# Scattering the rows of alternate expert tiles into two DRAM tensors, and adding the second to the first at the end

## What is computed

```python
x = x + xattn(ctx_1024, layernorm(x))            # 32 x 100 x 256, residual
z    = layernorm(x) * g + b
p    = softmax(z @ rW + rb)                       # 8 experts
topv, topi = top_k(p, 2)
w    = topv / sum(topv)                           # weights of the 2 experts of a row
hid  = gelu(z @ W1[e] + b1[e])                    # 256 -> 512, for each chosen e
y    = hid @ W2[e] + b2[e]                        # 512 -> 256
out  = x + sum over the 2 chosen e of w[e] * y
```

## Time and profile before

| | us |
|---|---|
| median of 3 runs | 854.98 |
| lowest and highest of the 3 | 854.52, 857.09 |
| the profiled execution: its own time | 857.09 |
| the profiled execution: span from first to last instruction | 855.3 |

### The profile page before, as it was taken

The page is one execution under the profiler, slowest core; times in us unless marked ns, Lnnn a source line. Parts: engine busy times, 40 slices in busy tenths (PEclk is TensorE's granted clock), DMA queues, the critical chain, the costliest instruction groups (busy, mean ns, idle before and its releaser), DMA issues.

```text
span 855.3 us, 26299 instructions
## 1 busy us (share of the span) xinstructions
PE 753.1 (88%) x8056; PEld 587.4 (69%) x8057; DVE 672.4 (79%) x1859; ACT 535.4 (63%) x1412; POOL 554.0 (65%) x610
## 2 busy tenths in 40 slices
PE   3389999999999999999999997655797698999994
PEld 2256677777777777777767675444687697988894
DVE  6389999999999999999999997993457865555562
ACT  2236788888888888888888885443363354554551
POOL 5432877777877777777778675433654457777773
PEclk9999999999999999999999999856999899999998
DMA  8846567677677576676776757611233233443341
GB/s 191 153 111 142 124 145 167 158 169 164 155 170 170 136 190 142 167 170 151 171 164 152 193 130 180 192 16 53 44 64 44 49 57 63 69 67 52 63 67 18
DMA packets 152792, 104.43 MB, mean 122 GB/s; under 512 B 68657, under 2 KB 147853, under 8 KB 152609
## 3 DMA queue, kind: packets, MB, share of 16 engines
q1 hardware_dynamic: 132598, 77.03, 39.6%
q0 software_dynamic: 11776, 16.15, 11.7%
q10 hardware_dynamic: 8362, 10.57, 4.3%
HBM read 36.65 MB, written 17.33 MB: 63 GB/s over the span
## 4 chain that ended last, share of the span: by engine, by line
PE 65%; DVE 15%; issue 7%; DMA 5%; DVEq 4%; POOL 3%; ACT 1%; ACTq 1%; POOLq 0%; SPq 0%
PE pj L863 10%; PE pj L832 9%; PE s_row L877 9%; PE zt L908 8%; PE s_t L896 8%; PE s_row L967 6%; DVE negmax L1336 3%; PE pj L850 3%; PE pj L978 3%; PE zt L978 2%; DMA q_stack<-q_part 2%; DVE v_neg L1442 1%; DVEq L1429 1%; DVEq L1437 1%; PE tr L932 1%
## 5 line engine op out<-in xcount | busy, mean ns | idle before, releaser
L1336 DVE TENSOR_REDUCE negmax<-s_row 100x1 f32<-100x361 f32 x512 | 251.4, 523 | 20.7 <-PE s_row L877 13.6
L1155 ACT ACTIVATE p_t<-s_t 128x400 f32<-128x400 f32 x384 | 188.6, 501 | 56.3 <-PE s_t L896 49.5
L877 PE MATMUL s_row<-stack_x,q_stack 125*128 125x361 bf16 x512 | 132.1, 320 | 15.7 <-DMA q_stack<-q_part 7.4
L703 POOL DMA_INDIRECT out_x<-v_neg,idx_s x57 | 94.2, 1652 | 75.6 <-DVE v_neg L1444 36.1
L896 PE MATMUL s_t<-q_stack,stack_x 128*128 128x100 bf16 x1536 | 128.7, 211 | 11.0 <-ACT p_t L1155 10.3
L896 PEld LDWEIGHTS s_t<-q_stack,stack_x 128*128 128x128 bf16 x1536 | 93.0, 99 | 57.3 <-issue 27.0
L967 PE MATMUL s_row<-w_qkv,v_aug 128*128 128x128 f32 x912 | 118.4, 285 | 13.7 <-DVE v_aug L1431 13.7
L967 PEld LDWEIGHTS s_row<-w_qkv,v_aug 128*128 128x128 f32 x912 | 111.6, 200 | 17.2 <-DVE v_aug L1431 14.8
L863 PE MATMUL pj<-w_qkv,ct 128*128 128x256 f32 x384 | 106.9, 402 | 0.0
L1141 ACT ACTIVATE w_qkv<-s_row,b_k 128x128 f32<-128x128 f32 x228 | 65.2, 369 | 63.0 <-PE s_row L967 63.0
L832 PE MATMUL pj<-ct,w_qkv 128*128 128x361 f32 x256 | 94.9, 494 | 10.8 <-DMA bk_s<-in_bk 9.7
(11 more groups left out here) (234 smaller groups left out, 1432.2 us busy)
## 6 DMA issues: line engine op xcount, KB each, us to landing
stack_x<-k_part SPq DMA_DIRECT2D x192, 192.0 KB, 3.8
q_stack<-q_part SPq DMA_DIRECT2D x186, 64.0 KB, 2.0
ct<-in_ctx_t SPq DMA_DIRECT2D x32, 361.0 KB, 4.9
stack_x<-in_w ACTq DMA_DIRECT2D x8, 512.0 KB, 6.2
w_s<-in_w ACTq DMA_DIRECT2D x14, 256.0 KB, 2.9
zscr<-zn SPq DMA_DIRECT2D x32, 100.0 KB
z_in<-zscr SPq DMA_DIRECT2D x32, 100.0 KB
zf_d<-zf_s SPq DMA_DIRECT2D x32, 100.0 KB
```

The lines of the kernel that those rows point to most:

```text
L703: pool.indirect_dma_start(out_rows[0:n], bass.IndirectOffsetOnAxis(idx_s[:, k.slot:k.slot + 1], 0), ys[:, k.slot, :], None, bounds_check=n ...
L877: nc.tensor.matmul(s_row[h % 2][:, 0:KEYS], q_stack[0:MROW, b.slot, h, :], k_stack[0:MROW, b.slot, h, 0:KEYS], start=True, stop=True).then ...
L1155: nc.scalar.activation(p_t[:, quad % 2, kt, :], s_t[g % 2][:, 0:4 * Q], ACT.Exp).then_inc(exp_done, 1)
L1336: v.tensor_reduce(negmax[:, b.slot, h:h + 1], s_row[h % 2][0:Q, 0:KEYS], AXIS.X, ALU.max, negate=True).then_inc(max_done, 1)
```

## The change

Scatters of even tiles still add to `out`; scatters of odd tiles now add to a second DRAM tensor, `odd_d`, of the same shape. Two transfers that follow each other thus never touch the same bytes, and scatters of one parity are ordered through DVE's step as before, so the wait on the other parity goes, together with the table `clear_at`, its two DVE instructions per group of tiles, its constants and POOL's register load. For this

- `odd_d` has to be zero at first: POOL writes 128 x 640 zeros over a dead part of `x_all` at the start of iteration 27, and ACT's queue sends them ten times over to `odd_d` (3.28 MB) at the start of iteration 29. ACT waits for that transfer at the start of iteration 31, POOL before the first scatter;
- at the end, after both parities have landed, POOL issues one DMA from DRAM to DRAM that adds all of `odd_d` to `out`, 400 rows of 2048 numbers (3.28 MB), and waits for it.

```diff
@@ zeroing (POOL, ACT)
+                    if isinstance(turn, int) and i == 27:
+                        pool.wait_ge(x2_stored, 16 * LOOSE)
+                        g.memset(zeros, 0.0).then_inc(zeros_ready, 1)
...
                 def load_weights(i):
+                    if i == 29:
+                        act.wait_ge(zeros_ready, 1)
+                        act.dma_start(odd_d.rearrange("b q d -> (b q d)").rearrange("(p r n) -> p r n", p=128, n=640),
+                                      zeros.unsqueeze(1).broadcast_to([128, B * Q * D // (128 * 640), 640])).then_inc(odd_zeroed, 16)
                     if i == 31:
+                        act.wait_ge(odd_zeroed, 16)
@@ first_gathers (POOL)
                     pool.wait_ge(x2_stored, 16 * LOOSE)
+                    pool.wait_ge(odd_zeroed, 16)
@@ scatter (POOL)
                 def scatter(k):
-                    other = scattered[1 - k.slot]
-                    if k.known and k.index in (3, NF):
-                        pool.wait_ge(clear_known, {3: 1, NF: 2}[k.index])
-                    if k.known and k.index in (0, 1, 2, NT - 1):
-                        after(pool, other, 16 * ((k.index + 1) // 2))
+                    if k.known:
+                        pool.wait_ge(y_ready, k.index + 1)
                     else:
-                        pool.reg_load(clear, clear_at[0:1, bass.ds(k.index, 1)])
-                        pool.wait_ge(other, clear)
-                    pool.wait_ge(y_ready, scatters[k.slot])
-                    pool.reg_add(scatters[1 - k.slot], scatters[k.slot], 1)
+                        pool.wait_ge(y_ready, scatters[k.slot])
+                        pool.reg_add(scatters[1 - k.slot], scatters[k.slot], 1)
                     n = rows_in(k)
-                    pool.indirect_dma_start(out_rows[0:n], ...
+                    pool.indirect_dma_start((out_rows, odd_rows)[k.slot][0:n], ...
@@ after the last scatter (POOL)
                 for k in range(2):
                     pool.wait_ge(scattered[k], 16 * len(range(k, NT, 2)))
+                wide = [t.rearrange("b q d -> (b q d)").rearrange("(r n) -> r n", n=2048) for t in (out, odd_d)]
+                pool.dma_start(wide[0], wide[1], accum_op=ALU.add, max_dma_last_dim=8192).then_inc(odd_added, 16)
+                pool.wait_ge(odd_added, 16)
@@ to_places (DVE)
-                    route(dve, v.tensor_tensor(same, te_i[:, mine], te_i[:, mine.start - 1:mine.stop - 1], ALU.is_equal))
-                    v.scalar_tensor_tensor(clear_at[0:Q, mine], same, -16.0, landed[:, mine.start - 3:mine.stop - 3], ALU.mult, ALU.add).then_inc(clear_known, 1)
```

More of the change, by code:

```diff
@@ L157, in build @@
 def build(nc, x, ctx_t, wq_t, bq, wk_t, bk, wv_t, bv, gamma, beta, ln_g, ln_b, rw, rb, w1, b1, w2, b2,
-          ident_d, route_c, zscr, zf_d, out):
+          ident_d, route_c, zscr, zf_d, odd_d, out):
     es = ExitStack()
@@ L224, in build @@
         ln0 = [ln0_all[:, k * B:k * B + B] for k in range(3)]
-        cst = stats_all[:, 0:E + 128 + 1 + NT - 3]
-        rev, lanes, query, landed = carve(cst, (E, 128, 1, NT - 3))
+        cst = stats_all[:, 0:E + 128 + 1]
+        rev, lanes, query = carve(cst, (E, 128, 1))
         ones, earlier = carve(ln0_all[:].bitcast(BF16), (Q, Q))
@@ L265, in build @@
         b2_s = ct[:].rearrange("p a c k -> p (a c k)")[:, 0:E * D].rearrange("p (e f) -> p e f", e=E)
-        w2_loaded, cst_loaded, clear_known = sem("w2_loaded"), sem("cst_loaded"), sem("clear_known")
+        w2_loaded, cst_loaded, odd_zeroed = sem("w2_loaded"), sem("cst_loaded"), sem("odd_zeroed")
         x2_late = sem("x2_late")
@@ L542, in build @@
             idx_t = [idx0, idx1]
-            clear_at = slot_c.bitcast(I32)
             zg = q_part[:].rearrange("p a s t k -> p (a s t k)")[:, 0:2 * 4 * ROW].bitcast(FP32).rearrange("p (r w) -> p r w", r=4)
@@ L556, in build @@
             scattered = [sem(f"scattered{k}") for k in range(2)]
+            zeros_ready, odd_added = sem("zeros_ready"), sem("odd_added")
             zgt_done, zgt_copied, up_done, b1_ready, gelu_done = (sem(k) for k in ("zgt_done", "zgt_copied", "up_done", "b1_ready", "gelu_done"))
@@ L559, in build @@
             w1_copied = sem("w1_copied")
+            zeros = stack_x[:, stack_words:stack_words + 640]
             N_W2 = 16 * (E + 1)
@@ L672, in _ @@
                 scatters = [pool.alloc_register(f"scatters{k}") for k in range(2)]
-                clear = pool.alloc_register("clear")
-                pool.reg_mov(scatters[0], 1)
                 zf_rows = zf_d.rearrange("b q d -> (b q) d")
                 out_rows = out.rearrange("b q d -> (b q) d")
+                odd_rows = odd_d.rearrange("b q d -> (b q) d")
                 def rows_in(k):
@@ L691, in scatter @@
                 def scatter(k):
-                    other = scattered[1 - k.slot]
-                    if k.known and k.index in (3, NF):
-                        pool.wait_ge(clear_known, {3: 1, NF: 2}[k.index])
-                    if k.known and k.index in (0, 1, 2, NT - 1):
-                        after(pool, other, 16 * ((k.index + 1) // 2))
-                    else:
-                        pool.reg_load(clear, clear_at[0:1, bass.ds(k.index, 1)])
-                        pool.wait_ge(other, clear)
-                    pool.wait_ge(y_ready, scatters[k.slot])
-                    pool.reg_add(scatters[1 - k.slot], scatters[k.slot], 1)
+                    if k.known:
+                        pool.wait_ge(y_ready, k.index + 1)
+                    else:
+                        pool.wait_ge(y_ready, scatters[k.slot])
+                        pool.reg_add(scatters[1 - k.slot], scatters[k.slot], 1)
                     n = rows_in(k)
-                    pool.indirect_dma_start(out_rows[0:n], bass.IndirectOffsetOnAxis(idx_s[:, k.slot:k.slot + 1], 0), ys[:, k.slot, :], None,
+                    pool.indirect_dma_start((out_rows, odd_rows)[k.slot][0:n], bass.IndirectOffsetOnAxis(idx_s[:, k.slot:k.slot + 1], 0), ys[:, k.slot, :], None,
                                             bounds_check=n - 1, oob_is_err=False, compute_op=ALU.add).then_inc(scattered[k.slot], 16)
@@ L790, in _ @@
                 pool.reg_mov(gathers[0], NF + 5)
+                pool.reg_mov(scatters[1], NF)
                 remaining(pool, tile_step, LOOP[0])
@@ L1412, in to_places @@
                     route(dve, v.tensor_tensor(it[1], it[1], it[0], ALU.add))
-                    mine = slice(max(sl.start, 3), sl.stop)
-                    same = slot_c[0:Q, mine]
-                    route(dve, v.tensor_tensor(same, te_i[:, mine], te_i[:, mine.start - 1:mine.stop - 1], ALU.is_equal))
-                    v.scalar_tensor_tensor(clear_at[0:Q, mine], same, -16.0, landed[:, mine.start - 3:mine.stop - 3], ALU.mult, ALU.add).then_inc(clear_known, 1)
                 def to_gather(k):
@@ L1646 @@
         "route_c": np.concatenate([np.tile(np.concatenate([np.arange(E, 0, -1), np.arange(128)]), (Q, 1)),
-                                   1 + np.arange(Q)[:, None], np.tile(16 * ((np.arange(3, NT) + 1) // 2), (Q, 1))], 1).astype(np.float32),
+                                   1 + np.arange(Q)[:, None]], 1).astype(np.float32),
     }
@@ L1652 @@
     args["zf_d"] = nc.dram_tensor("zf_d", [B, Q, ROW], FP32, kind="Internal").ap()
+    args["odd_d"] = nc.dram_tensor("odd_d", [B, Q, D], FP32, kind="Internal").ap()
     args["out"] = nc.dram_tensor("out_x", [B, Q, D], FP32, kind="ExternalOutput").ap()
```

2 lines of the change are left out of this document (1 added, 1 removed).

## The result

| | before | after |
|---|---|---|
| median (5 runs each) | 854.98 us | 876.82 us |
| lowest to highest | 853.56 to 857.09 | 874.43 to 878.76 |
| profiled execution, own time | 857.09 | 875.23 |
| its span | 855.3 | 873.4 |

The changed kernel takes 1.0235 times as long, with a 95% interval from 1.0207 to 1.0265. The forecast was 875.5 us with a range from 868 to 889, so the time came out 1.3 us above it.

A forecast was written before the change was run, and what follows sets the result against it. The prediction took PE to bound the tiles. The end -3.4 and adding transfer +21.4 make +18.0, plus zeroing +2.5 and tiles 0, +20.5 us on the median of 854.98: 875.5 us, range 868 to 889.

The forecast's parts named there:

- PE sets the pace in the tiles: Tiles, 683 to 836 us: PE is busy for 149.2 of 153.0 us, so POOL's 27.5 us of waits mostly cost nothing.
- Rival 5: All over the tiles: the removed waits held up gathers and PE; all 27.5 us freed would give 851.4 us; chance 0.02.
- The bounds of 0 and -3 for the tiles: Tiles, 590 to 842 us: taken as 0, with at most PE's whole pause before tile 24 gained, -3 us.
- The end: Last scatters: scatter 56 issues at 846.64 instead of 849.99, gaining 3.4 us, bounds 2 (the odd gap stays) and 4.
- Rival 4: Last scatters: the end doesn't move forward, held by DVE's wait or the gap before the last issue; 878.9 us; chance 0.04.
- The adding transfer: After the last landing: issue 0.3, fixed part 2.5 and data 18.6 us at 176 GB/s, 21.4 us with nothing hiding it.
- Rival 1: Adding transfer at the scatter's 103 GB/s: 31.8 us in place of 18.6, 888.7 us; chance 0.19 with what lies between.
- Rival 2: Adding transfer: the second read costs nothing, so it goes at 352 GB/s; 866.2 us; chance 0.07.
- The time of 863: Adding transfer: estimate by the skill page's formula, 2.0 us plus bytes over 436 GB/s, 9.5 us for everything.
- The zeroing: Around iteration 29: the zeros partly push back the last batch's keys, which PE awaits; +2.5 us, bounds 0 and 6.
- rival 3: Zeroing: the zeros collide with the last batch's keys in full and PE's clock falls; +6 us, 879.0 us; chance 0.06.
- the subtraction of 2.1 us: Sum: from the profiled execution's forecast, 877.6 us, to the median's, 875.5, because before's profiled execution was its slowest.

The follow-up runs named there:

- experiment 3: Experiment 2 without the adding transfer, so the odd tiles' rows are missing from the output: 851.86 us against 855.85, ratio 0.9957.
- experiment 12: The kernel before with all its waits, plus only the zeroing of the second tensor in iteration 29: 858.44 us against 855.81, ratio 1.0034.
- experiment 8: The kernel before, with scatter 56 waiting for scatter 53 and no longer for scatter 55: 853.13 us against 853.80, ratio 0.9985.
- 10: The changed kernel again, with no edit: 873.32 us against 855.81, ratio 1.0202.
- 1: The changed kernel without the last transfer from `odd_d` to `out`: 856.15 us against 855.85, ratio 0.9983.
- 5: The changed kernel with its last transfer regrouped to rows of 1 KB, which were joined again, so the same transfer ran: 875.18 us in one execution.
- experiment 6: The changed kernel with its last transfer as a plain copy of `odd_d` over `out`, not an add: 865.75 us in one execution.
- experiment 7: The changed kernel with its last transfer adding only the first half of `odd_d`, 200 rows of 8 KB: 862.16 us in one execution.
- experiment 9: The changed kernel with its last transfer cut into 3200 rows of 1 KB: 881.04 us in one execution.
- experiment 2: The changed kernel with the zeroing moved to iteration 32, from dead columns of `ct` in rows of 1 KB: 868.48 us against 855.85, ratio 1.0141.
- experiment 4: The changed kernel with the zeroing issued in slot 4 of iteration 29 in place of slot 0: 877.32 us against 855.85, ratio 1.0269.
- experiment 11: Experiment 2 with POOL writing its zeros one iteration earlier, in iteration 31: 877.60 us against 855.81, ratio 1.0255.

## Why the prediction held, step by step

**PE sets the pace in the tiles: right.** 27.5 us of idle time on POOL went without a change in PE's busy time between 683 and 836 us, in the kernel after and in experiment 3. The pause at tile 24 stayed, and from its end to PE's last large matmul the traces of kernels with the waits need 129.3 to 130.8 us (12, before, 8), and those without them 128.4 to 130.4 (128.84 in after, 129.07 in experiment 3). Rival 5, which needed 23.9 us, had at most 5.9 by experiment 3's interval. The bounds of 0 and -3 for the tiles were sensible: in the table, the seven executions with early zeros and without the waits (after, 10, 1, 5, 6, 7, 9) need 319.2 to 321.9 us from the last keys to PE's last matmul, and experiment 12, with the waits, 322.8. That hints at 1 to 3 us gained ahead of tile 24. But experiment 2, also without the waits, has 323.76 like the kernel before, and a part may be the clock: from 640 to 683 us it was granted at 0.90 in the trace of before and at 0.99 in that of after, and it was 0.88 to 1.00 in the other traces, in no order that follows the change. These rows don't separate the two, so this stays open.

**The end: mechanism right, size 1.0 us off.** The step that failed is "Scatter 56 then issues at 845.73 + 0.91". DVE's chain ran as told: `idx_s` waits for scatter 54's landing, the result is ready 846.41 + 0.35 = 846.76, 1.17 us after it (predicted 1.18). But from the result to the issue it took 2.04 us and not 0.91. The gap ahead of the last scatter that the prediction kept as a bound is real, and every kernel has it: 1.98 us in the chain of work of after (846.83 to 848.80), 1.97 us from the register move at 848.02 to the scatter at 849.99 before, and 1.97 us in experiment 8 (843.54 to 845.51). Other scatters need 0.8 to 0.9 from their result. The term is 2.4 us and not 3.4, inside its bounds. What causes the gap was not tried. Rival 4, that the end doesn't move, is out.

**The adding transfer: mechanism right, 2.2 us too dear.** Predicted 0.3 + 2.5 + 18.6 = 21.4 us, measured 0.3 + 3.3 + 15.6 = 19.2. The mis-sized term is the rate: "twice the reading at the rate of those large loads" gave 176 GB/s, and it is 210. The fixed part was 0.8 us larger than the scatter's rows gave. The reasons given against the scatter's pace and for the loads' (the weight of the first reads, many rows behind each other) were tested by no run; only the rates were. Rival 1 (31.8 us of data at the scatter's pace) fell with the first landing, and experiment 9 shows that even rows of 1 KB stay far from it. Rival 2 (9.3 us) fell with the same landing, and experiment 6 says why: the copy needs that much, the add doesn't. (The time of 863 that stands there for the page's formula should read 864: 875.5 - 21.4 + 9.5 = 863.6.)

**The zeroing: the size held by chance, the mechanism was wrong in its main step.** The prediction filled the free share of the DMA engines in time order and let the rest push back the keys, for +2.5 us, and named PE's first read of the last keys as the victim. What was late in fact was `m_part`, a transfer of 9.4 KB issued 0.27 us behind the zeros, with PE 3.57 us idle and then 4 us at 1.2 GHz; the keys were issued 4.65 us later (20.79 - 16.14), because SP needed 4.46 us more to issue `q_part` ahead of them, and by then PE was as late itself, so they caused no pause of their own. The failed assumption is that a free share of 74% means that small transfers pass: `m_part` landed 6.8 us after its issue, where 515.70 - 512.48 = 3.2 us had been enough before. Experiment 4 shows the predicted victim, with a pause of 6.27 us. Of the 4.65 us, 0.2 to 2.8 us are left at PE's last matmul in the seven executions with early zeros and without the waits (340.03 to 342.69 for 339.88), in which what the removed waits may have given back is included; with all waits in place, experiment 12 has 3.7 in its trace and 2.9 by its ratio. The sum's +2.5 was near that, and rival 3 (+6) lies outside experiment 12's interval.

The sum closes: three terms missed by +1.0 (end), -2.2 (add) and, in the profiled execution, -1.3 (front: 1.2 for 2.5), together -2.5, and the profiled execution took 875.23 where 877.6 was forecast. That the median is nevertheless above the forecast comes from the subtraction of 2.1 us with which the prediction went over to the medians: before's profiled run was its slowest, but after's was the second fastest of six. Over all 23 executions of the kernel after on record the median is 876.07, 0.6 us above the forecast.

## What to carry over

A second destination for alternate scatters costs one pass over the tensor at the end, where nothing hides it; it can pay only if the waits that it removes lie on the path for longer than that pass. Read this from the busy time of the engine that sets the pace, not from the idle time of the engine that waits: here 27.5 us of idle time held 3.7 us (1.5 to 5.9, the end included). A large transfer that "fits into the free share" is to be placed by what small transfers come right behind it, on any queue, and which engine waits for them: the same 3.28 MB showed no loss in front in experiment 2, cost 2.9 us in experiment 12, and 6.4 us more in the trace of experiment 11 than in that of 2, by where it was issued.

## What the runs showed that I had not expected

- An adding transfer from DRAM to DRAM moves 210 GB/s, a copy 351, both at a DMA share of 1.01. Of the add's 18.9 us, 3.3 don't go with the bytes (experiment 7).
- Behind a large transfer, SP's own issuing gets slow: six transfers of `q_part` took 8.93 us to issue instead of 4.47, six of `k_part` 9.51 instead of 3.83 (experiment 4). The engine that only issues is held up too.
- A round trip of 100 KB through DRAM took 14.6 us behind the zeros and 5.5 without them (experiments 11 and 2).
- The gap of about 2 us ahead of the very last scatter, in every kernel; its cause stays open.
- Experiment 8's edit, which the shown input allows, did not beat the kernel before measurably, and no kernel that does all of the work with two tensors came below 868.5 us. The best version stays the kernel before.
